# A four-layer image kernel: spline weights loaded and prepared earlier, value ranges taken per image, and sent rows counted on two semaphores

## The chip, the cores and the metric

The kernel runs on one core of one Trainium2 chip. The metric is the device time of one execution in microseconds (us). The engines are TensorE (PE; its weight loads are PEld), VectorE (DVE), ScalarE (ACT), GpSimd (POOL) and SyncE (SP), which here only issues DMAs.

## The reference

The input x is 8 images of 32 x 32 positions with 128 channels, so 8192 tokens. Four layers follow each other. Each adds two things to x: a mixer of the normalised x, and a mixture of experts of the again normalised sum. The mixers are a fractal measure (L0), an involution (L1), a spline network (L2) and an attention without softmax (L3). The layer that matters here is L2. Its mixer is, with `n` the normalised x:

```
x_min, x_max = min and max of n per channel over all 8192 tokens
u      = (n - x_min) / (x_max - x_min + 1e-7)
bases  = hat functions of u on a grid of 9 knots
spline = einsum(bases, spline_weight * spline_scaler)      # 128 x 128 x 9
out    = silu(bn_base(n @ base_weight)) + bn_spline(spline)
```

The minimum and the maximum go over all images, so no token's bases can be computed before the last image is normalised. Every layer's experts take each token's best expert (L0) or its best two (L1, L2, L3) of 8 (16 in L3), run a two-step network on it, and add the weighted results.

## The kernel before, in words

`build` (L2294) runs constants, then for each layer `norm_mixer` and the layer's mixer, then `finish`. Each of these is a block of its own: five programs, one per engine, that start together and are waited for together at the end, so a block's start stands behind its slowest engine.

`norm_mixer` (L249) first brings back the results of the layer before: SP loads them image by image (L276), GpSimd adds each token's two results (L284), VectorE adds them to the residual and takes statistics (L299, L301). When all 8 images are in, one square root on ScalarE (L332) and a reciprocal follow. Then the images are normalised in tiles of 128 tokens, 8 tiles per image: VectorE takes six (L313), ScalarE two (L339). TensorE turns each image so that channels lie on partitions (L326), and ScalarE copies it into `k.ch` (L347, or L349 where the image has no border).

`mixer_spline` (L1860) opens the next block. SP loads eight vectors of 128 numbers (`load_columns`, L1239), the base weight, the spline weight and its scaler, and waits for them; only then come the bias columns, the gate and the experts' weights. VectorE writes some constants (L1929, L1931), waits for the loads, scales the weights (L1935), derives from the 9 knots one slope and three bends (L1937 to L1941), a level at zero (L1943), the batch norm factors (L1949 to L1953) and the combined weights (L1955). TensorE turns these (L2026). VectorE then takes the channel's minimum and maximum over all 8192 tokens in two reductions (L1958, L1959), and works out the range, its inverse and the three bend positions (L1960 to L1963). After them come the bends of image 0 (`bends`, L1971) on VectorE and ScalarE's scaled copies of the turned weights (L2006), and TensorE starts on the images.

While a mixer works on image b, `Router` handles image b-1: its sum and norm, the choice of experts, and the slots into which its rows go (`place`, with the end of each image at L693 and L695). GpSimd then sends the rows to a buffer in device memory by indirect DMA, one DMA per tile and choice, 16 per image with two choices (`send_tile`, L795). The slots have two buffers, for even and odd images. All sends of a layer count on one semaphore, `rows_sent`, and `send` waits at the end of each image until all of them have landed:

```
    def send(self, pool, b):
        self.slots_known(pool, b)
        for t in range(TPB):
            self.send_tile(pool, b, t)
        pool.wait_ge(*self.when("rows_sent", 16 * TPB * self.K * (b + 1)))
```

`Experts` then works through tiles of 128 dispatched rows, 136 of them in L1 and L2, 144 in L3, in loops whose body spells out 16 tiles (`tiles`, L929 to L961). SP loads a tile's rows into one of 16 places (`load`, L965), and for this waits until the tile 16 before has been returned. TensorE turns it (L1004) and does the two products (L1012, L1022), ScalarE the activation (L1079, L1082), VectorE copies and weights the result (L1120, L1126, L1145), and GpSimd returns it by an indirect DMA (L1214). The last image is routed in between: its sends stand in GpSimd's program before the returns of certain tiles (in L2 from the thirteenth on, in L1 from the tenth on), and VectorE places it and plans the second part of the tiles between other tiles. SP writes pad rows (L493) between the loads of the third sixteen, then loads the second table (L500), waits for all rows sent and all pads, and goes on with the loads.

## Time and profile before

| | |
|---|---|
| runs | 2334.99, 2335.71, 2338.59 us (median 2335.71) |
| profiled execution, its own time | 2337.0 us |
| its span | 2335.2 us |
| granted TensorE clock, mean | 0.874 |
| busy: PE / PEld | 1749.2 us (75%) / 1376.5 us (59%) |
| busy: DVE / ACT / POOL | 1550.6 us (66%) / 1174.8 us (50%) / 983.7 us (42%) |
| DMA | 153.81 MB, 66 GB/s over the span |

The times are of whole executions. The span is what the hardware profiler saw from the first to the last instruction, 1.8 us less than the execution's own time. Busy shares are means over stages with different limits. In a timeline, each line has the start, the length, the engine, the line of the kernel, the operation, output and inputs, the shape and the number of instructions merged into it. In brackets stands how long the engine was idle before it, and what ended this.

### The profile page before, as it was taken

The page shows a single profiled execution, that of the slowest core. Times are in us where ns is not written, and L with a number is a line of the kernel's source. Part 1 is how long each engine was busy: PE and PEld are TensorE (multiplying, and loading weights), DVE is VectorE, ACT ScalarE, POOL GpSimd, SP SyncE. Part 2 cuts the span into 40 slices and gives each one's busy share as a digit, 9 for nine tenths or more (in the row PEclk, how much of TensorE's full clock was granted, in tenths as well). Part 3 has the DMA queues.
Part 4 walks back from the last instruction along what each step waited for, and adds up shares of the span by engine and source line. Part 5 has one row for each costly group of instructions (what it writes and reads, how often), then busy time and mean ns, then how long its engine had stood idle before and what let it go on. Part 6 is the DMA issues. An engine that isn't in the chain of part 4 may idle for free. (4 is left out here: it accounts for less than half of the span.)

```text
span 2335.2 us, 46315 instructions
## 1 busy us (share of the span) xinstructions
PE 1749.2 (75%) x10980; PEld 1376.5 (59%) x10981; DVE 1550.6 (66%) x4683; ACT 1174.8 (50%) x2635; POOL 983.7 (42%) x969
## 2 busy tenths in 40 slices
PE   1488666993588888999952566779719999888992
PEld 1133566893344345999951344667617777787992
DVE  6898886786577776654437676646576777754554
ACT  2445776893333334776642233546635444455661
POOL 0000233552013435764442077677640365466662
PEclk9799766997699999999985788779959999989996
DMA  2002002222200002232242012233243011123326
GB/s 74 1 0 60 26 27 56 78 69 83 74 12 26 32 23 65 76 93 63 60 136 75 11 51 76 64 94 102 78 145 109 19 38 33 52 70 96 92 77 220
DMA packets 183551, 153.81 MB, mean 66 GB/s; under 512 B 40290, under 2 KB 162818, under 8 KB 183358
## 3 DMA queue, kind: packets, MB, share of 16 engines
q1 hardware_dynamic: 153406, 92.37, 14.6%
q0 software_dynamic: 29952, 59.26, 7.5%
q8 instruction: 74, 1.21, 0.2%
q14 instruction: 119, 0.97, 0.2%
HBM read 85.33 MB, written 68.79 MB: 66 GB/s over the span
## 5 line engine op out<-in xcount | busy, mean ns | idle before, releaser
L1214 POOL DMA_INDIRECT returned<-rows_second_choice x488 | 482.4, 989 | 312.1 <-DVE rows_second_choice L1145 111.5
L1012 PE MATMUL psum<-rows_first_choice 128*128 128x128 f32 x3360 | 473.0, 282 | 8.1 <-DVE rows_first_choice L1126 8.1
L1022 PE MATMUL psum<-expert_weights,rows_first_choice 128*128 x2784 | 427.7, 290 | 61.7 <-ACT rows_first_choice L1079 17.3
L1012 PEld LDWEIGHTS psum<-rows_first_choice 128*128 128x128 f32 x3360 | 431.5, 199 | 10.1 <-DVE rows_first_choice L1126 9.9
L1022 PEld LDWEIGHTS psum<-expert_weights,rows_first_choice 128*128 128x128 f32 x2784 | 361.5, 197 | 99.8 <-issue 93.1
L795 POOL DMA_INDIRECT dispatched<-rows_first_choice,slot x192 | 191.6, 998 | 519.3 <-DVE rows_second_choice L695 409.2
L1079 ACT ACTIVATE rows_first_choice<-psum,bias_columns 128x128 f32<-128x128 f32 x1104 | 323.5, 368 | 171.9 <-PE psum L1012 153.8
L795 POOL DMA_INDIRECT dispatched<-rows_second_choice,slot x192 | 193.5, 1008 | 58.5 <-issue 58.2
L1120 DVE COPY rows_first_choice<-expert_weights 128x512 f32 (+1 forms) x272 | 105.8, 389 | 144.5 <-PE psum L1012 120.6
L326 PE MATMUL psum<-identity,rows_first_choice 128*128 128x128 f32 x256 | 41.5, 320 | 201.8 <-DVE rows_first_choice L313 190.3
L1145 DVE SCALAR_TENSOR_TENSOR rows_second_choice<-psum,rows_second_choice,rows_first_choice 128x128 f32<-128x128 f32 x344 | 119.4, 347 | 103.9 <-PE psum L1022 101.1
L795 POOL DMA_INDIRECT dispatched<-rows_first_choice,expert_weights x64 | 62.1, 970 | 267.5 <-DVE rows_first_choice L693 250.1
L1062 ACT ACTIVATE rows_first_choice<-expert_weights 128x512 f32 x216 | 136.8, 634 | 50.0 <-issue 49.9
L326 PEld LDWEIGHTS psum<-identity,rows_first_choice 128*128 128x128 f32 x256 | 34.9, 167 | 207.7 <-DVE rows_first_choice L313 190.7
L1126 DVE COPY rows_first_choice<-psum 128x128 f32<-128x128 f32 x488 | 137.2, 282 | 13.6 <-PE psum L1004 12.4
L1004 PE MATMUL psum<-identity,rows_second_choice 128*128 128x128 f32 x488 | 137.5, 283 | 7.9 <-DMA rows_second_choice<-dispatched 7.6
L1082 ACT ACTIVATE rows_first_choice<-rows_first_choice,rows_second_choice 128x128 f32 x344 | 141.2, 410 | 0.0
L1132 DVE TENSOR_TENSOR rows_first_choice<-rows_first_choice,psum 128x256 f32<-128x256 f32 x144 | 60.6, 421 | 113.8 <-ACT rows_first_choice L1072 106.5
L2214 PE MATMUL psum<-channel_major 128*128 128x512 f32 x256 | 131.7, 598 | 1.2 <-ACT channel_major L2132 1.2
L2148 ACT ACTIVATE att_work<-psum 128x512 f32<-128x512 f32 x128 | 73.1, 596 | 90.0 <-PE psum L2214 84.1
L2223 PEld LDWEIGHTS psum<-rows_second_choice,rows_first_choice 128*128 128x128 f32 x680 | 88.7, 191 | 47.0 <-issue 34.9
L2223 PE MATMUL psum<-rows_second_choice,rows_first_choice 128*128 128x128 f32 x680 | 90.3, 276 | 5.4 <-DVE rows_first_choice L2182 5.4
(369 smaller groups left out, 3274.6 us busy)
## 6 DMA issues: line engine op xcount, KB each, us to landing
rows_second_choice<-dispatched SPq DMA_DIRECT2D x488, 65.0 KB
expert_weights<-returned SPq DMA_DIRECT2D x12, 1024.0 KB, 10.3
rows_second_choice<-returned SPq DMA_DIRECT2D x8, 1024.0 KB, 10.6
returned<-rows_second_choice POOLq DMA_INDIRECT x488
expert_weights<-in_L_ffn_w SPq DMA_DIRECT2D x3, 2048.0 KB, 8.3
residual<-in_x SPq DMA_DIRECT2D x8, 512.0 KB, 7.2
rows_first_choice<-returned SPq DMA_DIRECT2D x4, 1024.0 KB, 8.9
out<-residual SPq DMA_DIRECT2D x8, 512.0 KB, 6.0
```

What stands on the lines that cost most here:

```text
L795: pool.indirect_dma_start(out=self.k.dispatched, out_offset=bass.IndirectOffsetOnAxis(ap=self.slot[:, b % 2, c, t:t + 1], axis=0), in_=sel ...
L1004: pe.transpose(k.ps[:, self.PSX + u % 2, 0:P], self.rt[:, u, 0:C], k.ident[:]).then_inc(self.s["x_turned"].h, 1)
L1012: ins = pe.matmul(k.ps[:, self.PSH + u % 2, j * P:(j + 1) * P], self.wc[:, u % 2, j * P:(j + 1) * P], self.xt[:, u % 2, :], start=True, st ...
L1022: ins = pe.matmul(self.result_bank(u), self.gs[:, u % self.HB, j * P:(j + 1) * P], self.second[:, bass.ds(e, 1), j, :].rearrange("p a c -> ...
L1062: act.activation(self.wc[:, u % 2, :], self.first[:, bass.ds(e, 1), :].rearrange("p a f -> p (a f)"), ACT.Copy).then_inc(self.s["w_copied" ...
L1079: ins = act.activation(self.hs[:, u % self.HB, cols], k.ps[:, self.PSH + u % 2, cols], f["act"], bias=self.bcol[:, bass.ds(e * self.J + j, ...
L1082: act.activation(self.wb[:, u % 4, :], self.b2rows[:, bass.ds(e, 1), :].rearrange("p a c -> p (a c)"), ACT.Copy, scale=self.rt[:, u, C + 1 ...
L1126: dve.tensor_copy(self.xt[:, u % 2, :], k.ps[:, self.PSX + u % 2, 0:P]).then_inc(self.s["x_copied"].h, 1)
L1145: ins = dve.scalar_tensor_tensor(out=self.ys[:, u, :], in0=self.result_bank(u), scalar=weight, in1=self.wb[:, u % 4, :], op0=ALU.mult, op1 ...
L1214: pool.indirect_dma_start(out=k.returned[0:N * self.K, :], out_offset=bass.IndirectOffsetOnAxis(ap=self.rt[:, u, C:C + 1].bitcast(I32), ax ...
L2214: pe.matmul(k.ps[:, g % 4, :], xft[:, b * IMG + j * P:b * IMG + (j + 1) * P], xft[:, b * IMG + h * BANK:b * IMG + (h + 1) * BANK], start=T ...
L2223: ins = pe.matmul(k.ps[:, 4 + h, t * P:(t + 1) * P], r2[g % 3][:, t * P:(t + 1) * P], val[:, b, j * P:(j + 1) * P], start=(j == 0 and t == ...
```

## The change

Four things are changed.

1. A new class `SplineWeights` holds the spline mixer's weights and small vectors. They are allocated ahead of layer 1's mixer, the large ones in a part of `rows_second_choice` behind image 6's start. Its `load` issues the eleven DMAs on SP; it is given to layer 1's `Experts` as `load_next`, which calls it behind the last tile's load and waits there for the landing.
2. Layer 2's `norm_mixer` is given these weights. VectorE does the arithmetic on them (`prepare`) ahead of the residual additions, ScalarE the two roots first, and TensorE turns the combined weights first.
3. In that block ScalarE normalises tiles 1, 2, 4, 5 and 7 of each image and VectorE the other three. VectorE takes the minimum and the maximum of each image once it is copied, two images behind its own tiles. The mixer only reduces the 8 minima and 8 maxima.
4. `rows_sent` becomes `even_sent` and `odd_sent`. `send` no longer waits for its own rows, but before an image for those of the image two before it. Whoever waited for all rows waits for both semaphores.

```diff
-def norm_mixer(k, layer):
+def norm_mixer(k, layer, spline=None):
...
+    by_scalar = (1, 2, 4, 5, 7) if spline else (3, 7)
...
+            if spline:
+                spline.prepare(dve)
             for b in range(B):
                 ch = Chain(dve, s["norm_step"], s["norm_step"].base + b * per)
...
+            def image_range(b):
+                dve.wait_ge(*when("turned_copied", b + 1))
+                spline.image_range(dve, b)
+
             for b in range(B):
-                for t in (b * TPB + j for j in range(TPB) if j % 4 != 3):
+                for t in (b * TPB + j for j in range(TPB) if j not in by_scalar):
                     ins = dve.tensor_scalar(k.xn[:, t, :], k.x[:, t, :], k.mean[:, t:t + 1], k.rstd[:, t:t + 1],
                                             ALU.subtract, ALU.mult)
                 ins.then_inc(s["norm_most"].h, 1)
+                if spline and b >= 2:
+                    image_range(b - 2)
+            if spline:
+                image_range(B - 2)
+                image_range(B - 1)
...
         def _(pe):
+            if spline:
+                spline.turn(pe)
...
         def _(act):
+            if spline:
+                spline.roots(act)
...
-                for t in range(b * TPB + 3, (b + 1) * TPB, 4):
+                for t in (b * TPB + j for j in by_scalar):
...
+    def sent(self, images, parity):
+
+        return self.when(("even_sent", "odd_sent")[parity], 16 * TPB * self.K * ((images + 1 - parity) // 2))
+
+    def all_sent(self, eng, images):
+        for parity in range(2):
+            eng.wait_ge(*self.sent(images, parity))
...
             if b >= 2:
-                dve.wait_ge(*self.when("rows_sent", 16 * TPB * K * (b - 1)))
+                dve.wait_ge(*self.sent(b - 1, b % 2))
...
-                in_=self.rows[c][:, b * TPB + t, :], in_offset=None).then_inc(self.s["rows_sent"].h, 16)
+                in_=self.rows[c][:, b * TPB + t, :],
+                in_offset=None).then_inc(self.s[("even_sent", "odd_sent")[b % 2]].h, 16)
...
     def send(self, pool, b):
         self.slots_known(pool, b)
+        if b >= 2:
+            pool.wait_ge(*self.sent(b - 1, b % 2))
         for t in range(TPB):
             self.send_tile(pool, b, t)
-        pool.wait_ge(*self.when("rows_sent", 16 * TPB * self.K * (b + 1)))
...
         route.load_table(sp, 0)
-        sp.wait_ge(*route.when("rows_sent", 16 * TPB * self.K * route.first_images))
+        route.all_sent(sp, route.first_images)
...
         route.load_table(sp, 1)
-        sp.wait_ge(*route.when("rows_sent", 16 * TPB * self.K * B))
+        route.all_sent(sp, B)
...
         for t in range(self.T // RING * RING, self.T):
             load(t, t % RING)
+        if self.load_next:
+            self.load_next(sp)
...
                 route.slots_known(pool, B - 1)
+                pool.wait_ge(*route.sent(B - 2, (B - 1) % 2))
...
+class SplineWeights:
...
+    def load(self, sp):
+        i, sem = self.k.ins, self.s["spl_loaded"]
+        load_columns(sp, sem, self.vec, [i[f"L2_conv_bn_{a}_{b}"] for a in ("base", "spline")
+                                         for b in ("gamma", "beta", "mean", "var")])
+        sp.dma_start(self.base_w[:], i["L2_conv_base_weight"]).then_inc(sem.h, 16)
+        sp.dma_start(self.spw[:], i["L2_conv_spline_weight"]).then_inc(sem.h, 16)
+        sp.dma_start(self.scl[:], i["L2_conv_spline_scaler"]).then_inc(sem.h, 16)
+        sp.wait_ge(*self.when("spl_loaded", 16 * 11))
...
+    def image_range(self, dve, b):
+        image = self.k.ch[:, b * IMG:(b + 1) * IMG]
+        dve.tensor_reduce(self.ranges[:, 0, b:b + 1], image, AX.X, ALU.min).then_inc(self.s["spl_ranged"].h, 1)
+        dve.tensor_reduce(self.ranges[:, 1, b:b + 1], image, AX.X, ALU.max).then_inc(self.s["spl_ranged"].h, 1)
...
-            ch.note(dve.tensor_reduce(rng[:, 0:1], k.ch[:, 0:N], AX.X, ALU.min))
-            ch.link(dve.tensor_reduce(rng[:, 1:2], k.ch[:, 0:N], AX.X, ALU.max))
+            dve.wait_ge(*weights.when("spl_ranged", 2 * B))
+            ch.note(dve.tensor_reduce(rng[:, 0:1], weights.ranges[:, 0, :], AX.X, ALU.min))
+            ch.link(dve.tensor_reduce(rng[:, 1:2], weights.ranges[:, 1, :], AX.X, ALU.max))
```

`prepare`, `roots` and `turn` hold the same operations on the weights as `mixer_spline` had, in the same order, with their scratch room in `rows_first_choice`.

## Rows read from the trace of the kernel before

**Rows 1.** The head of the page: the whole span.
```profile
span 2335.2 us, 46315 instructions
```

**Rows 2.** Windows: stretch, length, busy of PE, PEld, DVE, ACT, POOL, clock, DMA.
```profile
1265.00:1300.00 35.00, 1.19 (x5) 0.79 (x5) 26.06 (x36) 1.87 (x8) 0.00 (x0) 0.51 0.29 82
...
1600.00:1660.00 60.00, 57.38 (x419) 47.64 (x418) 37.70 (x139) 42.22 (x139) 44.84 (x46) 1.00 0.37 103
```

**Rows 3.** Timeline of VectorE, norm block of L2 and the mixer's preparation.
```profile
1218.87 3.36 DVE L299 TENSOR_TENSOR residual<-residual,expert_weights 128x1024 f32<-128x1024 f32 x1 [17.35 <-POOL expert_weights L284]
...
1248.92 12.39 DVE L313 TENSOR_SCALAR rows_first_choice<-residual,mean,rstd 128x128 f32<-128x128 f32 x48
1265.48 0.29 DVE L1929 MEMSET hats_at_zero<- 128x1 f32 x9 [4.17 <-PEq L264]
...
1273.83 1.36 DVE L1935 TENSOR_TENSOR spline_w<-spline_w,spline_scaler 128x1152 f32<-128x1152 f32 x1 [7.98 <-DMA spline_scaler<-in_L_conv_spline_scaler]
...
1280.66 8.68 DVE L1958 TENSOR_REDUCE channel_range<-channel_major 128x1 f32<-128x8192 f32 x1
1289.26 8.68 DVE L1959 TENSOR_REDUCE channel_range<-channel_major 128x1 f32<-128x8192 f32 x1
1297.97 0.16 DVE L1960 TENSOR_TENSOR channel_range<-channel_range 128x1 f32<-128x1 f32 x1
...
1298.73 2.08 DVE L1971 TENSOR_SCALAR expert_weights<-channel_major,bends 128x1024 f32<-128x1024 f32 x3
```

**Rows 4.** Timeline of ScalarE in the same norm block.
```profile
1249.04 1.65 ACT L339 ACTIVATE rows_first_choice<-residual,four_variances,rstd 128x128 f32<-128x128 f32 x4 [0.95 <-DVE four_variances L309]
1252.61 1.03 ACT L349 ACTIVATE channel_major<-psum 128x1024 f32<-128x1024 f32 x1 [1.92 <-PE psum L326]
1253.53 0.87 ACT L339 ACTIVATE rows_first_choice<-residual,four_variances,rstd 128x128 f32<-128x128 f32 x2
1254.31 1.03 ACT L349 ACTIVATE channel_major<-psum 128x1024 f32<-128x1024 f32 x1
...
1264.12 1.02 ACT L349 ACTIVATE channel_major<-psum 128x1024 f32<-128x1024 f32 x1 [0.29 <-PE psum L326]
```

**Rows 5.** Timelines of SP and GpSimd, end of L1 and start of the norm block.
```profile
1129.24 45.70 SPq L965 DMA_DIRECT2D rows_second_choice<-dispatched  x24
1206.79 5.78 SPq L276 DMA_DIRECT2D expert_weights<-returned  x4
...
1216.51 2.33 POOL L284 TENSOR_TENSOR expert_weights<-expert_weights 128x1024 f32<-128x1024 f32 x1 [13.73 <-issue]
```

**Rows 6.** Timeline of GpSimd in L2: sends and the first returns.
```profile
1335.90 1.42 POOL L795 DMA_INDIRECT dispatched<-rows_first_choice,slot  x1 [95.04 <-DVE rows_second_choice L695]
...
1467.23 0.96 POOL L795 DMA_INDIRECT dispatched<-rows_first_choice,slot  x1 [1.60 <-DMA dispatched<-rows_second_choice,slot]
...
1489.37 1.00 POOL L1214 DMA_INDIRECT returned<-rows_second_choice  x1 [2.10 <-DMA dispatched<-rows_second_choice,slot]
...
1505.54 1.00 POOL L1214 DMA_INDIRECT returned<-rows_second_choice  x1 [0.30 <-issue]
1506.85 1.07 POOL L795 DMA_INDIRECT dispatched<-rows_first_choice,slot  x1 [0.30 <-issue]
```

**Rows 7.** Timeline of VectorE in L2: image 6's slots, the twelfth tile's result.
```profile
1462.41 0.17 DVE L695 TENSOR_TENSOR rows_second_choice<-weight_sum,exponentials 128x8 f32<-128x8 f32 x1
...
1502.14 0.35 DVE L1145 SCALAR_TENSOR_TENSOR rows_second_choice<-psum,rows_second_choice,rows_first_choice 128x128 f32<-128x128 f32 x1
```

**Rows 8.** Timeline of SP in L2: tile loads around the pads.
```profile
1538.72 1.66 SPq L965 DMA_DIRECT2D rows_second_choice<-dispatched  x2
...
1563.24 109.22 SPq L965 DMA_DIRECT2D rows_second_choice<-dispatched  x88
```

**Rows 9.** Timeline of GpSimd in L1: the ninth return.
```profile
948.59 0.98 POOL L1214 DMA_INDIRECT returned<-rows_second_choice  x1 [1.48 <-DVE rows_second_choice L1145]
```

**Rows 10.** Timeline of ScalarE in L1's experts: the first of two such gaps.
```profile
1086.03 1.14 ACT L1079 ACTIVATE rows_first_choice<-psum,bias_columns 128x128 f32<-128x128 f32 x4 [5.38 <-issue]
```

More of the change, by code:

```diff
@@ L882, with __init__ @@
     HB = 4
-    def __init__(self, k, layer, ctx, route):
+    def __init__(self, k, layer, ctx, route, load_next=None):
         nc, f = k.nc, FFN[layer]
+        self.load_next = load_next
         self.k, self.layer, self.f, self.route, self.tail = k, layer, f, route, TAILS[layer]
@@ L1611, in mixer_fractal, with mixer_involution @@
     route.done()
-def mixer_involution(k):
+def mixer_involution(k, load_next):
     nc, i = k.nc, k.ins
@@ L1872, in mixer_spline @@
+def mixer_spline(k, weights):
+    nc = k.nc
+    BENDS, TERMS = weights.BENDS, weights.TERMS
+    base_w, bn, bend, level = weights.base_w, weights.bn, weights.bend, weights.level
+    names = ("spl_v", "spl_wcopied", "spl_shift", "spl_basis", "spl_level", "spl_base", "spl_used", "spl_silu", "spl_mixed")
     s = {n: k.sem(n) for n in names}
@@ L1904, in _ @@
         def _(sp):
-            load_columns(sp, s["spl_loaded"], vec, [i[f"L2_conv_bn_{a}_{b}"] for a in ("base", "spline")
-                                                    for b in ("gamma", "beta", "mean", "var")])
-            sp.dma_start(base_w[:], i["L2_conv_base_weight"]).then_inc(s["spl_loaded"].h, 16)
-            sp.dma_start(spw[:], i["L2_conv_spline_weight"]).then_inc(s["spl_loaded"].h, 16)
-            sp.dma_start(scl[:], i["L2_conv_spline_scaler"]).then_inc(s["spl_loaded"].h, 16)
-            sp.wait_ge(*when("spl_loaded", 16 * 11))
             ex.sync_early(sp)
@@ L1946, in _ @@
-            dve.wait_ge(*when("spl_root", 2))
-            for j in range(2):
-                g, bt, mn = (vec[:, 4 * j + a:4 * j + a + 1] for a in range(3))
-                ch.link(dve.reciprocal(bn[:, j, 1:2], bn[:, j, 0:1]))
-                ch.link(dve.tensor_tensor(bn[:, j, 1:2], bn[:, j, 1:2], g, ALU.mult))
-                ch.link(dve.tensor_tensor(bn[:, j, 2:3], bn[:, j, 1:2], mn, ALU.mult))
-                ch.link(dve.tensor_tensor(bn[:, j, 2:3], bt, bn[:, j, 2:3], ALU.subtract))
-            ch.note(dve.scalar_tensor_tensor(out=level[:, 0:1], in0=level[:, 0:1], scalar=bn[:, 1, 1:2], in1=bn[:, 1, 2:3],
-                                             op0=ALU.mult, op1=ALU.add))
@@ L1999, in _ @@
         def _(act):
-            act.wait_ge(*when("spl_loaded", 16 * 11))
-            for j in range(2):
-                act.activation(bn[:, j, 0:1], vec[:, 4 * j + 3:4 * j + 4], ACT.Sqrt, bias=k.eps3).then_inc(s["spl_root"].h, 1)
             act.wait_ge(s["spl_v"].h, s["spl_v"].base + k.spline_pre)
-            act.wait_ge(*when("spl_wturned", 1))
+            act.wait_ge(*weights.when("spl_wturned", 1))
             for t in range(TERMS):
-                act.activation(spt[:, t, :], k.ps[:, 4, t * P:(t + 1) * P], ACT.Identity,
+                act.activation(spt[:, t, :], k.ps[:, weights.BANK, t * P:(t + 1) * P], ACT.Identity,
                                scale=rng[:, 2:3]).then_inc(s["spl_wcopied"].h, 1)
@@ L2023, in _ @@
         def _(pe):
-            pe.wait_ge(*when("spl_combined", 1))
-            for t in range(TERMS):
-                ins = pe.transpose(k.ps[:, 4, t * P:(t + 1) * P], combined[:, t, :], k.ident[:])
-            ins.then_inc(s["spl_wturned"].h, 1)
             pe.wait_ge(*when("spl_wcopied", TERMS))
@@ L2273, in build @@
         constants(k)
-        mixers = [mixer_fractal, mixer_involution, mixer_spline, mixer_attention]
-        for layer in range(4):
-            norm_mixer(k, layer)
-            mixers[layer](k)
+        norm_mixer(k, 0)
+        mixer_fractal(k)
+        norm_mixer(k, 1)
+        with ExitStack() as spline_ctx:
+            weights = SplineWeights(k, spline_ctx)
+            mixer_involution(k, weights.load)
+            norm_mixer(k, 2, weights)
+            mixer_spline(k, weights)
+        norm_mixer(k, 3)
+        mixer_attention(k)
         finish(k)
```

109 lines of the change are left out of this document (71 added, 38 removed).

## The prediction

> **What bounds the kernel now.** I read the page's head first: one core, 2335.2 us of span [rows 1]. The profiled execution took 2337.0 us, 1.8 more than its span; the median of the runs is 2335.71, 1.3 below it. The sum is made against the profiled execution and carried over to the median as it is. No engine is full over the whole span, so what a part of the change is worth must be read stage by stage, and the second view is the table of windows around the third layer (L2), where nearly all of the change lies [rows 2]. In it two things stand out. From 1265 to 1300 us TensorE does 1.19 us of work in 35 and GpSimd nothing: that is the spline mixer's preparation, and the whole kernel stands behind it. From 1600 to 1660 GpSimd returns 46 tiles, one per 1.30 us, while TensorE is busy for 57.38 of 60: there the expert stage is limited by two engines at once.
>
> The third view is VectorE's timeline of the preparation [rows 3]. The reader is to see one unbroken sequence: block start at 1265.48, 7.98 us of idling until the last weight lands, 6.8 us of small work on the weights (1273.83 to 1280.66), two reductions of all 8192 columns, four small operations (0.76 us, 1297.97 to 1298.73), and then the first bends. Nothing else runs, so 33.25 us from block start to bends is critical.
>
> **Part 1: weights loaded behind layer 1's tiles.** Eleven DMAs go onto SP's queue behind the last tile load. SP issues its last tile load of layer 1 by 1174.94 (1129.24 + 45.70) and is next needed at 1206.79 [rows 5]. From the mixer's start to the landing of the last of the eleven went 8.4 us, 1265.48 to 1273.83 [rows 3]; the hole has 31.9. Cost 0. If the cover were gone, at most those 8.4 us would return. The load ring's tiles are issued ahead, so no tile load stands behind them.
>
> **Part 2: the weights' arithmetic in the norm block.** VectorE now idles 17.35 us until 1218.87, waiting for the first image's rows to come back and be added by GpSimd [rows 3]. The block starts at about 1206.8, SP's first issue [rows 5]. Twelve memsets 0.4 us, then 6.8 to 6.9 us of arithmetic: done at 1214.1, 4.8 us before VectorE is wanted, 2.4 us before GpSimd's first addition at 1216.51 [rows 5]. ScalarE's two roots and TensorE's four transposes run while both are idle; bank 4 is not used by the norm. Cost 0, gain: 1265.48 to 1280.66, that is 15.2 us, leaves the path.
>
> The Trainium skill speaks of what happens if the cover is missed: in its page SBUF — State Buffer, section on SBUF's two separate sides, a VectorE operation with two SBUF inputs and a GpSimd operation that reads SBUF exclude each other for their whole duration. The trace agrees in that the first residual addition, beside GpSimd's second, took 3.36 us [rows 3].
>
> **Part 3: the norm block's new split and the ranges.** ScalarE normalises 5 tiles of an image, not 2; VectorE 3, not 6, and takes each image's minimum and maximum. ScalarE's pace: two tiles take 0.78 us from start to start (1253.53 to 1254.31), so 0.39 each; two tiles and a copy of an image take 1.70 (1252.61 to 1254.31), so the copy's share is 0.92 [rows 4]. From 1249.04: ten tiles 3.9 us, first copy from 1253.0 to 1254.0; then 5 x 0.39 + 0.92 = 2.87 us per image; the seventh copy starts at 1270.2, the eighth is over by 1272.4 after its transposes.
>
> VectorE: a tile costs 12.39/48 = 0.26 us [rows 3], so 24 tiles 6.2 us. A reduction of 1024 columns isn't in the trace. From below it costs 8.68/8 = 1.08; from above 1024/1152 of the 1.36 us of L1935, 1.21 [rows 3]. I take 1.13: 1024 columns at 1.06 ns, 0.14 us fixed (L1935's 1.36 less 1152 x 1.06), less the 0.08 by which neighbours overlap (1280.66 to 1289.26 is 8.60, not 8.68). Sixteen make 18.1. VectorE does three images' tiles by 1251.3, waits for the first copy until 1254.0, and then is the later of the two engines: 1248.92 + 6.2 + 18.1 + 2.7 = 1275.9. Both ends of the reduction's cost give 1275.1 and 1277.2.
>
> The skill's page VectorE: DVE Perf Modes, section on the TRN2 errata, speaks against cutting one large reduction into eight: SBUF operations pay a fixed extra latency per instruction. By its (N+151)/0.96 a reduction would take 1.22 us and sixteen 19.6, so the block would end at 1277.4; no run here shows this shape.
>
> After the block: about 0.3 us to the next (it was 1265.14, the end of the last copy, to 1265.48) [rows 3, 4], two reductions over 8 numbers some 0.3 together, then the same four operations, 0.76. Bends start at 1277.3 and not at 1298.73: **21.4 us gained**. What is late next is nothing new: ScalarE's copies of the turned weights wait for the same ranges as before. The gate's and experts' loads now start with the block, at 1276.3, rather than once the spline weights had landed, about 1273.8, and are wanted from 1300 on. Cost 0, and at most a microsecond or two if the gate's weights were late.
>
> **Part 4: two semaphores for sent rows.** Before, GpSimd stood after each image's sends until all had landed. Layer 0, 1 and 3: images come slower than they are sent, so the wait hides, except the one before the first returned tile (about 2.1 us less 0.3 of normal spacing). In layer 1 the ninth tile then waits 1.48 us for VectorE's result anyway [rows 9], so nothing is left; I cost layers 0 and 3 at 0 by the same pattern, at most 1.8 us each.
>
> Layer 2 is different. There GpSimd is never idle by more than these waits: sends from 1335.90, a gap at each of the six image changes, 1.60 us before image 6, and 2.10 before the first return at 1489.37 [rows 6]. Sixteen sends take 1489.37 - 2.10 - 1467.23 = 20.0 us. Image 6's slots were ready at 1462.58 [rows 7] but its sends began at 1467.23. Without the waits they begin at 1462.9, end at 1482.9, and the first return comes at 1483.3, 6.1 us early. But from the first to the twelfth return took 16.2 us [rows 6], so the twelfth would go at 1499.5, and its result is only there at 1502.49, after VectorE has placed image 7 and planned the second half [rows 7]. So it goes at 1502.8, not 1505.54: **2.7 us** remain. They do pass on: image 7's sends (from 1506.85) set the pace of returns, these free the ring's tiles, SP's loads follow them until 1540 and from there SP's own chain of pads leads to the second table and the load at 1563.24 [rows 6, 8]. SP's and VectorE's new waits are for things long past.
>
> Sum: 21.4 + 2.7 = 24.1. From 2337.0 to 2312.9; against the median 2335.71, **2311.6**.
>
> **Rivals.**
> (a) The full 6.1 us pass through, because image 7's work on TensorE and VectorE also moves up: 27.5, 2308.2. For it: GpSimd has no other idle time in the layer. Against: that work waits for nothing from GpSimd. 0.10.
> (b) Nothing of the 2.7 comes through: GpSimd's sends now begin together with the bends on VectorE, and the one send that did so took 1.42 us, not 0.96 [rows 6]; or TensorE is the bound later. 21.4, 2314.3. 0.11.
> (c) The arithmetic doesn't fit under the return of rows, or the loads don't fit behind the tiles: 3 to 8 us back, 2315 to 2320. 0.05.
> (d) Slower. In layer 1 ScalarE twice stood for 5.4 us at a jump back of the expert loop, waiting for nothing in the program ("issue") [rows 10]; in layers 2 and 3 it never does. If this hangs on where the loop's code lies, the change moves it: ScalarE's program is longer by 24 activations ahead of both loops. These loops jump back 4 times in layer 2 and 5 in layer 3. All nine would cost 9 x 5.4 = 48.6 us less 24.1: 2360. It decides from the fifth jump on (27.0 > 24.1). All or most: 0.04. One to three of them, 2317 to 2328: 0.04.
> (e) The change doesn't do what it says: something else holds the mixer's start or the time comes back in the expert stage where two engines are full; within 4.7 us of 2335.7. 0.03.
>
> **How the numbers follow.** My forecast has 0.63, the rivals the rest. 0.2% of this time, 4.7 us, is about what a measurement of this kernel can tell from no change. Faster by more: 0.63 + 0.10 + 0.11 + 0.05 + 0.04 = 0.93; same 0.03; slower 0.04. Low end: rival (a) 2308.2 less the reduction at its cheap end (0.8) and 1.8 us of layer 0 or 3, 2305.6, rounded to 2305. High end: the forecast with the dear reduction (1.3), without the 2.7, and with one reload of 5.4: 2321.
>
> **What would show it.** Right: in the changed profile VectorE's spline arithmetic lies in the gap before the first residual addition, which starts no later than 12.1 us after the block; bends follow the norm block's end by 1.4 us and come 28.5 us after the normalisation starts, where it was 49.8; GpSimd's first send of each layer 2 image comes 0.4 us after its slots; its first return comes 6 us earlier against the mixer's start, its first send of image 7 under 3. Wrong: reductions of over 1.25 us, VectorE late for the first addition, sends of 1.4 us throughout, ScalarE gaps over 4 us at jumps in layers 2 or 3, or an expert stage longer by what the mixer gained.

## The result and the profile after

| | before | after |
|---|---|---|
| median of the runs beside each other | 2337.15 us | 2304.15 us |
| ratio, 95% interval | | 0.9859 [0.9845, 0.9874] |
| profiled execution, its span | 2335.2 us | 2301.3 us |
| norm block of L2, first DMA to first bends | 91.9 us | 70.7 us |
| first bends to image 6's slots | 163.8 us | 161.2 us |
| image 6's slots to the next norm block | 229.8 us | 222.9 us |
| next norm block to the end | 642.9 us | 639.9 us |

The table's stretches run from event to event. The norm block of L2 starts at SP's first load of returned rows; "image 6's slots" is the end of VectorE's row that writes the weights of its first choices (L693 before, L718 after). The row of the second choices, which the prediction took, ends 0.08 us later.

The change gains 33.0 us by the medians. The forecast was 24.1 and 2311.6; the range reached down to 2305, and the result lies 0.85 us below it. A second comparison gave 2303.55 against 2334.55, ratio 0.9874 [0.9857, 0.989], so 31.0. Of the table's rows the first three differences are 21.3, 2.6 and 6.9 us. The last row is the spread of profiles: kernels that keep all the old waits had 638.6 and 640.1 there (warm_before, warm_before2).

The head of the page of after:

```profile
span 2301.3 us, 46320 instructions
```

SP's timeline at the end of L1, which answers to [rows 5]: the eleven loads follow the last tile at once, and the last is issued over 25 us before SP is next needed.

```profile
1174.98 1.40 SPq L1270 DMA_DIRECT2D spline_vectors<-in_L_conv_bn_base_gamma  x1
...
1180.70 0.42 SPq L1933 DMA_DIRECT2D rows_second_choice<-in_L_conv_spline_scaler  x1
1206.72 8.75 SPq L277 DMA_DIRECT2D expert_weights<-returned  x5
```

VectorE's timeline of the norm block and the start of the mixer, which answers to [rows 3]:

```profile
1206.80 0.29 DVE L1944 MEMSET hats_at_zero<- 128x1 f32 x9 [5.32 <-PEq L1669]
...
1213.76 0.48 DVE L1971 TENSOR_SCALAR rows_second_choice<-rows_second_choice,spline_bn 128x512 f32<-128x512 f32 x1
1218.70 3.35 DVE L302 TENSOR_TENSOR residual<-residual,expert_weights 128x1024 f32<-128x1024 f32 x1 [4.46 <-POOL expert_weights L285]
...
1254.08 1.22 DVE L1988 TENSOR_REDUCE image_ranges<-channel_major 128x1 f32<-128x1024 f32 x1 [2.94 <-ACT channel_major L366]
1255.21 1.21 DVE L1989 TENSOR_REDUCE image_ranges<-channel_major 128x1 f32<-128x1024 f32 x1
1256.34 0.85 DVE L321 TENSOR_SCALAR rows_first_choice<-residual,mean,rstd 128x128 f32<-128x128 f32 x3
...
1274.82 1.21 DVE L1989 TENSOR_REDUCE image_ranges<-channel_major 128x1 f32<-128x1024 f32 x1
1276.36 0.16 DVE L2038 TENSOR_REDUCE channel_range<-image_ranges 128x1 f32<-128x8 f32 x1 [0.32 <-PEq L265]
...
1277.38 2.08 DVE L2051 TENSOR_SCALAR expert_weights<-channel_major,bends 128x1024 f32<-128x1024 f32 x3
```

The weights' arithmetic is over 4.46 us before the first residual addition (and 2.1 before GpSimd's first addition at 1216.34). The residual addition has not moved against the block's start (12.0 us; 12.1 before). From the first copy on VectorE has no idle time until the block ends. Its bends come 1.35 us after the block's last reduction, 28.6 us after the normalisation starts, where the forecast had 1.4 and 28.5.

GpSimd's timeline at image 6 of L2, which answers to [rows 6]:

```profile
1438.89 0.96 POOL L820 DMA_INDIRECT dispatched<-rows_first_choice,slot  x1 [0.47 <-DVE rows_second_choice L720]
...
1457.98 0.96 POOL L820 DMA_INDIRECT dispatched<-rows_second_choice,slot  x1 [0.30 <-issue]
1459.24 1.00 POOL L1245 DMA_INDIRECT returned<-rows_second_choice  x1 [0.30 <-issue]
1460.54 1.00 POOL L1245 DMA_INDIRECT returned<-rows_second_choice  x1 [0.31 <-issue]
...
1474.09 0.98 POOL L1245 DMA_INDIRECT returned<-rows_second_choice  x1 [0.91 <-DVE rows_second_choice L1175]
1475.38 0.97 POOL L820 DMA_INDIRECT dispatched<-rows_first_choice,slot  x1 [0.31 <-issue]
```

GpSimd now waits for the slots (released by VectorE's L720), not for its own rows, and its first send comes 0.34 us after image 6's slots at 1438.55. Counted from image 6's slots, the first return comes 6.2 us earlier than before (20.7 after 26.9), the first send of image 7 7.5 us earlier (36.8 after 44.3). The forecast had 6.1 and 2.7. The twelfth return, at 1474.09, is the only one among these that waits for VectorE, and it loses 0.6 us.

### The profile page after: what moved, and what is told of

The parts are those of the page before. It is cut to its first block and busy times, and to the rows that moved or that the text cites. A ratio compares the mean times of both kernels' runs of the same rounds, so it can differ in the third digit from the quotient of the medians.

```text
span 2301.3 us, 46320 instructions
## 1 busy us (share of the span) xinstructions
PE 1745.5 (76%) x10964; PEld 1375.2 (60%) x10981; DVE 1545.8 (67%) x4675; ACT 1183.7 (51%) x2659; POOL 981.1 (43%) x969
## 3 DMA queue, kind: packets, MB, share of 16 engines
q8 instruction: 74, 1.21, 0.2%
## 5 line engine op out<-in xcount | busy, mean ns | idle before, releaser
L820 POOL DMA_INDIRECT dispatched<-rows_second_choice,slot x192 | 187.7, 978 | 58.5 <-issue 58.2
L1156 DVE COPY rows_first_choice<-psum 128x128 f32<-128x128 f32 x488 | 137.4, 282 | 10.9 <-PE psum L1034 10.2
L2296 PEld LDWEIGHTS psum<-rows_second_choice,rows_first_choice 128*128 128x128 f32 x680 | 88.7, 191 | 47.0 <-issue 34.9
```

The source lines that it names most:

```text
L820: pool.indirect_dma_start(out=self.k.dispatched, out_offset=bass.IndirectOffsetOnAxis(ap=self.slot[:, b % 2, c, t:t + 1], axis=0), in_=sel ...
L1156: dve.tensor_copy(self.xt[:, u % 2, :], k.ps[:, self.PSX + u % 2, 0:P]).then_inc(self.s["x_copied"].h, 1)
L2296: ins = pe.matmul(k.ps[:, 4 + h, t * P:(t + 1) * P], r2[g % 3][:, t * P:(t + 1) * P], val[:, b, j * P:(j + 1) * P], start=(j == 0 and t == ...
```

## The experiments

"Stage 1" is the stretch from the norm block's start to the first bends, "stage 2" from there to image 6's slots, "stage 3" from there to the next norm block; all in L2, from each kernel's profile. In each set the kernel before ran beside them.

| kernel | median us | ratio, 95% interval | stage 1 | stage 2 | stage 3 |
|---|---|---|---|---|---|
| before | 2334.4 to 2337.2 | | 91.9 | 163.8 | 229.8 |
| after | 2304.15 | 0.9859 [0.9845, 0.9874] | 70.7 | 161.2 | 222.9 |
| after_again | 2303.55 | 0.9874 [0.9857, 0.989] | 70.7 | 161.1 | 222.5 |
| sems_only | 2328.42 | 0.9974 [0.9964, 0.9985] | 91.9 | 163.8 | 221.5 |
| all_waits | 2314.49 | 0.9915 [0.9898, 0.9931] | 70.7 | 160.9 | 230.8 |
| first_waits | 2311.85 | 0.9904 [0.9888, 0.9921] | 70.6 | 161.2 | 229.4 |
| last_wait | 2308.23 | 0.9895 [0.9879, 0.9912] | 70.5 | 161.3 | 224.1 |
| whole_range | 2311.5 | 0.9905 [0.9888, 0.9921] | 76.7 | 162.1 | 221.4 |
| old_split | 2306.86 | 0.9883 [0.9866, 0.9899] | 74.0 | 161.2 | 222.0 |
| load_in_norm | 2313.79 | 0.9912 [0.9896, 0.9929] | 80.8 | 161.2 | 222.1 |
| long_prepare | 2325.15 | 0.9962 [0.9949, 0.9974] | 88.4 | 163.9 | 221.9 |
| warm_before | 2334.68 | 1.0001 [0.9988, 1.0014] | 91.8 | 163.3 | 231.5 |
| warm_before2 | 2331.63 | 0.999 [0.9981, 1.0] | 92.2 | 159.8 | 230.1 |
| warm_after2 | 2303.67 | 0.9871 [0.9855, 0.9888] | 70.4 | 161.3 | 222.0 |

Stage 3 tells the two kinds apart at once: 229.4 to 231.5 where the waits at the image changes stand, 221.4 to 222.9 where no old wait is left; last_wait, with the one ahead of the first return, has 224.1.

### The sends: where did 6.9 us come from, when 2.7 was the forecast?

Two theories stood against each other. A: the whole cost of the waits passes on. B, the forecast's: the twelfth tile's result caps it.

**sems_only.** The kernel before with part 4 alone: `even_sent` and `odd_sent`, and no wait behind an image's own sends.

> The kernel before with the two semaphores alone. Two theories stand after the changed profile. A: the semaphores are worth all that GpSimd is ahead in L2, 4.4 us at image 6's sends, 1.8 at the first return, and 1.9 more at the second return, which no longer stands 2.2 us; the twelfth result is in time for this. Then image 7's first send comes about 8 us earlier against the bends' start than before, and with up to 2 us in L3 the kernel takes 2327 to 2329, 8 to 10 under before (2337.15). B, as predicted: the twelfth result caps it, 2.7 us, 2334.4; the rest of the 33 us then comes from the spline part.

Stage 3 fell from 229.8 to 221.5, 8.3 us; the median by 6.1 (2328.42 beside 2334.52), for which theory A had 8 to 10 and B 2.7. The part is worth this much without any help from the rest of the change. In the eight profiles without the old waits stage 3 lies between 221.4 and 222.9, so its price is known to about 1.5 us.

**all_waits, first_waits, last_wait.** The changed kernel with the wait for its own rows put back, on the two semaphores, behind every image, behind images 0 to 5 alone, or behind image 6 alone:

```diff
         for t in range(TPB):
             self.send_tile(pool, b, t)
+        self.all_sent(pool, b + 1)        # all_waits
...
+        if b < B - 2:                     # first_waits; last_wait has b == B - 2
+            self.all_sent(pool, b + 1)
```

> The changed kernel with GpSimd's wait for its own rows back at the end of each image (both semaphores). Theory A: 8 to 10 us over the changed kernel (2304.15), 2312 to 2314, and the bends still start within 0.3 us of where they do now against the norm block's start. Theory B: 2.7 over it, 2306.9. If the parts add up, this and the run of the semaphores alone are equally far from their neighbours.

> The changed kernel with the waits back behind images 0 to 5, none ahead of the first return. Theory A: image 6's sends in L2 begin some 4.4 us later and all that follows too, without either gap at the returns: 2308 to 2309. Theory B: capped by the twelfth result, at most 1 us over the changed kernel, 2305.

> The changed kernel with the wait back at one place only, behind image 6's sends and ahead of the first return. If the 2.2 us ahead of the second return belong to this wait, both gaps come back in every layer: first return of L2 1.8 us later, second 3.7, and the whole some 3.7 to 5 over the changed kernel, 2308 to 2309. If the second gap has another cause, it stays away and the whole is 1.8 over, 2306.

All of the waits cost 7.9 us of stage 3, those between images alone 6.5, the one ahead of the first return 1.2. By the medians the three kernels stand 10.3, 7.7 and 4.1 us above the changed kernel's 2304.15; A had expected 8 to 10, some 4.4 and 3.7 to 5, so it missed first_waits. So the cost is in the main an accumulated lag. In the kernel before, sixteen sends and their spacing take 20.3 us (16 x 1.27), with the gap of 1.6 to the next image 21.9, and an image comes every 21.2 (127.0 us for six). Each standstill pushes the following image's sends back, until image 6 starts 4.7 us after its slots.

The waits put back on two semaphores are longer than the old ones. The kernel before has gaps of 1.6 to 1.8 us at the image changes behind the first; in first_waits and all_waits every second gap is 2.1 to 2.4, and image 6's sends begin 7.3 and 7.4 us after its slots, not 4.7. So 6.5 and 7.9 are too high as prices of the old waits. GpSimd's row of image 6's first send in first_waits:

```profile
1446.90 1.02 POOL L820 DMA_INDIRECT dispatched<-rows_first_choice,slot  x1 [2.36 <-issue]
```

B falls: with the waits between images put back the twelfth return came 6.5 us later than in the changed kernel (from image 6's slots: 42.0 after 35.5).

GpSimd's timeline of last_wait shows what else the wait ahead of the returns does:

```profile
1458.84 0.96 POOL L820 DMA_INDIRECT dispatched<-rows_second_choice,slot  x1 [0.31 <-issue]
1461.89 1.00 POOL L1247 DMA_INDIRECT returned<-rows_second_choice  x1 [2.10 <-DVE rows_second_choice L1177]
1464.71 0.99 POOL L1247 DMA_INDIRECT returned<-rows_second_choice  x1 [1.82 <-issue]
1466.01 0.98 POOL L1247 DMA_INDIRECT returned<-rows_second_choice  x1 [0.30 <-issue]
```

There are two gaps and not one: 2.10 us ahead of the first return, which is the wait, and 1.82 ahead of the second, for which the profile names nothing in the program ("issue"). In the kernel before, the second is 2.2 us in L1, L2 and L3; there the profile names VectorE's L1145 in L1 and L2, but in L2 the second tile's result had been ready since 1476.49, 16 us earlier; in the changed kernel and in first_waits both gaps are gone in these layers (0.30). Behind a wait between images the next send follows after 0.3 us.

### The norm block: is each part worth what the sum said?

Theory C, in these expectations, is that the mixing is shorter after the change because TensorE enters it at a higher clock; the section after this one is on it.

**whole_range.** The changed kernel with part 3 undone: tiles 3 and 7 for ScalarE, no ranges in the norm block, two reductions of 8192 columns in the mixer.

```diff
-    by_scalar = (1, 2, 4, 5, 7) if spline else (3, 7)
+    by_scalar = (3, 7)
...
-            dve.wait_ge(*weights.when("spl_ranged", 2 * B))
-            ch.note(dve.tensor_reduce(rng[:, 0:1], weights.ranges[:, 0, :], AX.X, ALU.min))
-            ch.link(dve.tensor_reduce(rng[:, 1:2], weights.ranges[:, 1, :], AX.X, ALU.max))
+            ch.note(dve.tensor_reduce(rng[:, 0:1], k.ch[:, 0:N], AX.X, ALU.min))
+            ch.link(dve.tensor_reduce(rng[:, 1:2], k.ch[:, 0:N], AX.X, ALU.max))
```

> The changed kernel with part 3 undone: ScalarE normalises tiles 3 and 7 again, no ranges in the norm block, and the mixer takes two reductions of all 8192 columns. By my sum part 1 and 2 are worth 15.2 us and part 3 6.2 us, so the first bends should come 70.7 + 6.1 = 76.8 us after the norm block's start, and the whole time should rise by 6.1 us over the changed kernel. Theory C (clock) adds up to 1.7 to 2.6 us of slower mixing, because TensorE stands idle for 17 us again ahead of its first product: 6.1 to 8.7 in all, and bends to image 0's slots back near 36.8. Rival D (layout, loads): mixing stays at 35.1 and the rise is 6.1. A third outcome, under 4 us, would say that the ranges per image were worth less than the sum says.

Stage 1 is 76.7 us: parts 1 and 2 took 15.2 off the 91.9 and part 3 another 6.0, as summed (15.2 and 6.2). Stage 2 grew by 1.0, less than the 1.7 to 2.6 that theory C allowed, and image 0's slots came 35.6 us after the bends, between the rival's 35.1 and theory C's 36.8. The median stands 7.3 above the changed kernel.

**old_split.** Only the first two lines of that diff; VectorE takes 48 tiles and the ranges.

> The changed kernel with only the split of the normalisation undone: VectorE does six tiles of an image, ScalarE two; the ranges per image stay. VectorE is the later engine at the block's end, so 24 more tiles of 0.26 us, 6.2 us, lie on it; of these part is taken out of its waits for the first copy (2.7 us in the sum). Expected: bends 3.5 us later against the norm block's start than in the changed kernel (70.7 to 74.2), whole time 3.5 us longer. Rival: if ScalarE's copies, and not VectorE, had set the end (the last copy ended 3 us before VectorE's last reduction), nothing to 1 us.

Stage 1 grew by 3.3 us and the median by some 3. VectorE is the later engine, and moving tiles to ScalarE is worth the 6.2 us of the tiles less the wait for the first copy.

**load_in_norm.** Part 1 undone: the eleven loads are issued at the start of the norm block.

```diff
         def _(sp):
+                if spline:
+                    spline.load(sp)
...
-        sp.wait_ge(*self.when("spl_loaded", 16 * 11))
...
-            mixer_involution(k, weights.load)
+            mixer_involution(k, None)
```

> The changed kernel with part 1 undone alone: the eleven loads are issued by SP at the start of layer 2's norm block, ahead of the loads of the returned rows, and not behind layer 1's last tile. By the preparation of the kernel before, the last of the eleven lands about 8 us after the first is issued, the arithmetic of 6.8 us then ends some 15 us after the block's start instead of 7.4, and the loads of rows behind them are issued 3 to 4 us later. VectorE's first residual addition came 11.9 us after the block's start. Theory: bends come 3 to 7 us later (70.7 to 74 to 78), because both the arithmetic and the returned rows are late, and the time rises by as much. Rival: the rows' way over GpSimd takes up both, since the residual additions wait for it anyway: under 2 us. Third, as in the run with the longer preparation: the arithmetic falls beside GpSimd's additions, each blocks the other, and 8 us or more appear.

The third outcome: stage 1, from the first of the eleven at 1207.93, is 80.8, 10.1 us longer, and the median 10.2 longer than the changed kernel beside it. VectorE's timeline:

```profile
1216.36 1.36 DVE L1951 TENSOR_TENSOR rows_second_choice<-rows_second_choice 128x1152 f32<-128x1152 f32 x1 [7.99 <-DMA rows_second_choice<-in_L_conv_spline_scaler]
...
1221.10 0.16 DVE L1965 RECIPROCAL spline_bn<-spline_bn 128x1 f32<-128x1 f32 x1
1221.29 2.10 DVE L1966 TENSOR_TENSOR spline_bn<-spline_bn,spline_vectors 128x1 f32<-128x1 f32 x1
1223.42 2.27 DVE L1967 TENSOR_TENSOR spline_bn<-spline_bn,spline_vectors 128x1 f32<-128x1 f32 x1
1225.72 2.27 DVE L1968 TENSOR_TENSOR spline_bn<-spline_vectors,spline_bn 128x1 f32<-128x1 f32 x1
1228.03 0.16 DVE L1965 RECIPROCAL spline_bn<-spline_bn 128x1 f32<-128x1 f32 x1
1228.23 0.16 DVE L1966 TENSOR_TENSOR spline_bn<-spline_bn,spline_vectors 128x1 f32<-128x1 f32 x1
1228.42 2.33 DVE L1967 TENSOR_TENSOR spline_bn<-spline_bn,spline_vectors 128x1 f32<-128x1 f32 x1
...
1231.24 2.47 DVE L1972 TENSOR_SCALAR rows_second_choice<-rows_second_choice,spline_bn 128x512 f32<-128x512 f32 x1
```

And GpSimd's beside it:

```profile
1220.24 7.74 POOL L287 TENSOR_TENSOR expert_weights<-expert_weights 128x1024 f32<-128x1024 f32 x3 [16.30 <-DMA expert_weights<-returned]
1228.39 2.34 POOL L287 TENSOR_TENSOR expert_weights<-expert_weights 128x1024 f32<-128x1024 f32 x1 [0.41 <-DMA expert_weights<-returned]
```

An operation on one number per partition with two operands takes 0.16 us, and 2.10 to 2.33 while GpSimd adds; the reciprocal with one operand takes 0.16 even then, and the two-operand one at 1228.23 takes 0.16 in GpSimd's gap from 1227.98 to 1228.39. One instruction with a single tensor, the 128x512 at 1231.24, was held up too: 2.47 us beside an addition, 0.48 in the changed kernel. The Trainium skill, SBUF — State Buffer, section on SBUF's two separate sides, describes this as an exclusive lock between a two-input VectorE operation and a GpSimd operation that reads SBUF, held for the whole instruction. The trace agrees in both directions: none of the held-up instructions is much longer than one addition (2.34 us), and GpSimd's first three additions, the first of them started beside a 128x1152 of VectorE (L1959), took 7.74 us where three of 2.34 make 7.0.

The five held-up instructions lost 10.3 us together. But the run also moved something else: the loads of the returned rows stand behind the eleven, 5.1 us later, and GpSimd's first addition came 12.3 us after the block's first issue, not 9.6. The 10.1 us of the stage hold both effects, and no run here parts them.

**long_prepare.** The changed kernel with eight more multiplications of 128x1152 in `prepare`:

```diff
+        for _ in range(8):
+            ch.settle()
+            ch.note(dve.tensor_tensor(junk.rearrange("p (c t) -> p c t", t=KN), spw[:],
+                                      scl[:].unsqueeze(2).to_broadcast([P, C, KN]), ALU.mult))
```

> The changed kernel with eight more multiplications of the shape of the spline weight by its scaler (128x1152, 1.36 us each) in the preparation ahead of the residual additions, 11 us in all (with their waits 11 to 12). VectorE idled 4.46 us there, so this much is hidden and 6.5 to 7.5 us should appear: bends at 77 to 78 us after the norm block's start, whole time 6.5 to 7.5 us longer. Rival: because VectorE's arithmetic and GpSimd's additions would now fall together, and the first residual addition beside one of GpSimd's took 3.35 us where the others take about 1.1, they slow each other: then over 8 us. Second rival: the residual additions wait image by image for GpSimd, so a late start is caught up again and under 4 us appear.

Stage 1 grew by 17.7 us (the median by 21.0, with 2.7 more from stage 2), where 6.5 to 7.5 would have been the arithmetic alone: the eight took 19.19 us together instead of 11, and four of the small ones 2.06 to 2.26 each.

```profile
1212.81 19.19 DVE L1963 TENSOR_TENSOR rows_first_choice<-rows_second_choice 128x1152 f32<-128x1152 f32 x8
1231.92 0.15 DVE L1968 RECIPROCAL spline_bn<-spline_bn 128x1 f32<-128x1 f32 x1
1232.11 2.10 DVE L1969 TENSOR_TENSOR spline_bn<-spline_bn,spline_vectors 128x1 f32<-128x1 f32 x1
```

In the changed kernel GpSimd's first addition starts 9.6 us after the block, at 1216.34. Up to there arithmetic was free in these runs; behind it a two-operand instruction took about as long as one addition, however small it was, as long as GpSimd had no gap. (The expectation gives about 1.1 us for the other residual additions; the rows have 1.21 to 1.69.)

### The mixing: why 2.6 us shorter?

Windows of the first 14 us of mixing, before and then after; the third number from the end is TensorE's granted clock (1.00 is 2.4 GHz, 0.50 is 1.2 GHz):

```profile
1298.70:1305.70 7.00, 5.36 (x8) 2.68 (x9) 2.65 (x15) 3.38 (x6) 0.00 (x0) 0.50 0.01 2
1305.70:1312.70 7.00, 6.95 (x15) 2.62 (x13) 0.00 (x0) 1.54 (x2) 0.00 (x0) 0.92 0.00 0
```

```profile
1277.40:1284.40 7.00, 5.40 (x10) 2.77 (x11) 2.63 (x15) 3.67 (x7) 0.00 (x0) 0.62 0.49 103
1284.40:1291.40 7.00, 5.55 (x14) 2.10 (x12) 1.34 (x2) 1.22 (x1) 0.00 (x0) 1.00 0.55 203
```

The clock leaves its lower level earlier after the change. Over all fourteen profiles the first image follows this clock, and so does stage 2 but for warm_after2:

| granted clock, first 7 us of mixing | kernels | bends to image 0's slots | stage 2 |
|---|---|---|---|
| 0.50 | before, sems_only, long_prepare, warm_before | 36.8 | 163.3 to 163.9 |
| 0.55 | whole_range | 35.6 | 162.1 |
| 0.61 to 0.64 | after, after_again, all_waits, first_waits, last_wait, old_split, load_in_norm | 35.0 to 35.2 | 160.9 to 161.3 |
| 1.00 | warm_before2 | 33.5 | 159.8 |
| 1.00 | warm_after2 | 33.6 | 161.3 |

**warm_before** and **warm_before2.** The kernel before with 60, then 138 turns of the identity matrix ahead of TensorE's wait for the scaled weights, their results unused:

```diff
+            for t in range(138):
+                pe.transpose(k.ps[:, 7, (t % 4) * P:(t % 4 + 1) * P], k.ident[:], k.ident[:])
             pe.wait_ge(*when("spl_wcopied", TERMS))
```

> The kernel before, with 60 turns of the identity matrix given to TensorE just ahead of its wait for the four scaled spline weights (into a bank nothing else uses then), so that it works through the stretch in which it stood idle. The question is where the 1.7 us (to image 0's slots) and 2.6 us (to image 6's) come from by which the changed kernel's mixing is shorter, counted from the first bends. Theory C, the clock: TensorE enters the mixing at a higher granted clock; then bends to image 0's slots falls from 36.8 to about 35.1 us, bends to image 6's slots from 163.8 to 161 to 162.5, and the whole time by 1.5 to 2.6 us. Rival D, it is the memory layout (weights and scratch in other places) or the loads that start earlier: both stretches stay within 0.3 us of 36.8 and 163.8, and the whole time within 1 us of the kernel before.

> The kernel before with 138 turns of the identity matrix ahead of TensorE's wait for the scaled spline weights, where the run before this one had 60: those ended 9.4 us before the first product, the clock was back at 0.50 by then, and nothing was told apart. At the 0.107 us that the last of the 60 took, 138 end about 1 us before the scaled weights come. Theory C (the clock at which the mixing starts sets its length): granted clock 0.9 to 1.0 in the first 7 us of the mixing where it was 0.50, bends to image 0's slots 33.5 to 35.5 instead of 36.8, bends to image 6's slots at most 161.5 instead of 163.8. Rival: the mixing does not hang on the first 7 us of clock, 36.8 and 163.8 stay within 0.4.

The 60 missed their aim: they ended 9.4 us too early, the clock stood at 0.50 again when mixing began, and both stretches were near those of before (36.8 and 163.3). The 138 reached it, and windows of warm_before2 show the full clock:

```profile
1299.60:1306.60 7.00, 5.43 (x16) 2.50 (x14) 2.63 (x15) 4.90 (x7) 0.00 (x0) 1.00 0.00 0
1306.60:1313.60 7.00, 5.55 (x20) 2.81 (x19) 2.86 (x4) 0.00 (x0) 0.00 (x0) 1.00 0.00 0
```

Bends to image 0's slots fell from 36.8 to 33.5, stage 2 from 163.8 to 159.8. The median fell by 2.9 us, with an interval that reaches up to no change (0.9981 to 1.0). So the clock at the start is enough to move stage 2 by more than the change did. The rival, layout or earlier loads, falls with long_prepare: it has the changed kernel's layout and loads, and its mixing took 36.8 and 163.9, at 0.50 and 0.91 in the first two windows. Why the clock rises earlier in the changed kernel stays open: TensorE's work of the last 30 us before the bends is the same in long_prepare and in the changed kernel, the granted clock of the last 10 is 0.50 in both, and only in the 7 us behind the bends do they part (0.50 and 0.62).

**warm_after2** and **after_again.** The changed kernel with TensorE kept at work: 36 turns of the identity ahead of the first image's turns, 8 behind those of images 1 to 6, 36 behind the last, 16 ahead of the scaled weights; and the changed kernel itself.

```diff
             if spline:
                 spline.turn(pe)
+                pe.wait_ge(*when("norm_step", (B - 1) * per))
+                warm(36)
...
                 ins.then_inc(s["turned"].h, 1)
+                if spline and b:
+                    warm(8 if b < B - 1 else 36)
```

> The changed kernel with TensorE kept at work from the end of the statistics on: 36 turns of the identity before the first image's turns, 8 behind those of each of images 1 to 6, 36 behind the last, 16 ahead of the scaled spline weights. Theory C: the granted clock is near 1.00 when mixing starts (0.62 in the changed kernel's first 7 us), image 0's slots come 33.5 to 34.5 us after the bends instead of 35.1, and the whole time falls by 0.5 to 1.5 us against the changed kernel beside it. Rival: the extra turns delay the copies of the first images, VectorE gets its ranges later, and the norm block grows by 1 to 2 us, so that nothing is won or the time is longer by up to 2 us.

> The changed kernel itself, once more, beside the others of this call: 2304 us, and as a second profile the same stage lengths as the first within 0.3 us in layer 2 (norm block's start to bends 70.7, bends to image 6's slots 161.2, image 6's slots to the next norm block 222.9 with up to 2.5 of scatter, as the runs so far show in that stretch).

Image 0's slots came 33.6 us after the bends, 1.4 earlier, and image 6's at 161.3, no earlier at all; 2303.67 against 2303.55. The windows of warm_after2 tell where it was given back: behind the first 20 us the clock falls, while TensorE still has its work of images 0 and 1. In the second and third window below it is 0.82 and 0.54; the changed kernel has 1.00 and 0.61 in the same windows from its bends. Image 1's slots are level again, 55.5 us after the bends for 55.4.

```profile
1291.40:1299.80 8.40, 8.40 (x21) 3.64 (x20) 6.89 (x28) 2.79 (x3) 0.00 (x0) 1.00 0.00 0
1299.80:1306.00 6.20, 3.12 (x25) 2.76 (x23) 1.59 (x8) 3.25 (x3) 0.00 (x0) 0.82 0.00 0
1306.00:1314.80 8.80, 5.93 (x23) 3.82 (x24) 8.29 (x26) 1.54 (x2) 2.42 (x2) 0.54 0.02 8
```

No version that was run beats the changed kernel.

## Why the prediction was right or wrong

**Parts 1 to 3: right.** 21.4 us were forecast, 21.3 measured (91.9 to 70.7), and whole_range splits them as the sum did. The reduction of 1024 columns took 1.21 us, at the upper of the two bounds, but the next starts 1.13 after it, which is the number that the sum used: the last one ended at 1276.03 for 1275.9. The Trainium skill, VectorE: DVE Perf Modes, section on the TRN2 errata, gives (N+151)/0.96 ns for an addition of two fp32 tensors, not for a reduction; the prediction's 1.22 us is an estimate worked out from it. The trace agrees with it for one reduction (1.21 to 1.22 us); taken sixteen times in a row it gave a block end of 1277.4, 1.4 too late, since it has no overlap in it.

**Part 4: wrong, and the larger of two errors that together took the result out of the range.** The forecast let the first return come 6.1 us earlier (6.2 measured) and then held the twelfth back for its result "only there at 1502.49", which left 2.7. VectorE's timeline of the kernel before has these rows in that stretch:

```profile
1498.11 0.34 DVE L1145 SCALAR_TENSOR_TENSOR rows_second_choice<-psum,rows_second_choice,rows_first_choice 128x128 f32<-128x128 f32 x1
...
1502.14 0.35 DVE L1145 SCALAR_TENSOR_TENSOR rows_second_choice<-psum,rows_second_choice,rows_first_choice 128x128 f32<-128x128 f32 x1
```

The row at 1502.14, on which the step stood [rows 7], is the thirteenth tile's result. The twelfth's is the one before it, ready at 1498.45, ahead of the plan and not behind it, and a return at 1499.5 would have found it. Counting the rows of L1145 from the first tile of the layer shows it, and was not done. The thirteenth's return stands behind the first two sends of image 7 and waits just 0.2 us longer than its neighbours after the change. So the full 6.1 passed. With stage 3's measured 6.9 in place of 2.7 the forecast would have been 2307.4, still inside its range of 2305 to 2321; it took the next term as well to leave it. This has the size of rival (a), not its mechanism: image 7's slots came 34.9 us after image 6's, for 35.6 before, so that work hardly moved, and nothing needed it to.

**What stood in no term.** The second gap behind the wait, 2.2 us, went as well: the sum took over the 16.2 us from the first to the twelfth return as they stood, with the gap among them. 6.2 and 1.9 less the 0.6 that the twelfth return now waits make the 7.5 us by which image 7's sends start earlier; 6.9 are left at the end of the stage. And the mixing gave 2.6 us, through the clock by the experiments above, for which the forecast had neither a term nor a rival; 2307.4 less 2.6 is 2304.8. The forecast's 24.1 and these errors of 4.2 (6.9 less 2.7) and 2.6 make 30.9; the three stages show 30.8. What is left of the 33.0 is within the spread of the comparison (31.0 in the second).

**Rivals.** (b) and (c) needed sends of 1.4 us or late arithmetic; nearly all sends took 0.96 us (1.22 to 1.42 for the first of images 0, 4 and 5) and the arithmetic had 4.5 us to spare. load_in_norm and long_prepare show that (c), 3 to 8 us, was priced too low: there missing the cover cost 10.1 and 17.7 us, in good part because arithmetic and additions exclude each other. (d), code of ScalarE's loops: its gaps of 5.4 us stayed at two, both in L1, and none came in L2 or L3. (e) falls with the result. SP's loads behind L1's tiles cost nothing, as forecast.

**The range.** Its low end took in rival (a) and a cheap reduction, but no gain from the clock, though TensorE's clock stood at 0.51 in the very rows that were read [rows 2].

## What to carry to other kernels

A standstill at the end of each round on an engine that is nearly as slow as the rounds adds up over the rounds: price it by how far the last round starts behind its inputs, and let the gain pass unless a result is shown to be late, its row found by counting from the first. Where work is moved under a wait on VectorE, the cover for two-operand operations ended here at GpSimd's first addition, not at VectorE's own next instruction. Removing an idle stretch ahead of TensorE can also change the clock at which the next stage begins; take a bound for that from rows at either clock.

## What was unexpected of the hardware

- Behind a wait of GpSimd for its own sends, the first return was 2.1 us late and the second again, by 2.2 us (1.8 with the wait on two semaphores). The second gap came only where the wait stood ahead of returns, in L1, L2 and L3 with two choices; in L0 and behind waits between images the next gap was 0.3. The cause is open. The waits on two semaphores between images were longer at every second change (2.1 to 2.4 us for 1.6); that cause is open too.
- A VectorE operation with two operands of one number per partition took 2.06 to 2.33 us instead of 0.16 beside a GpSimd addition; a reciprocal beside it took 0.16.
- TensorE's granted clock at the start of mixing was 0.50, 0.55, about 0.62 or 1.00 in different kernels. It was worth up to 3.3 us on the first image and up to 4.0 on the stage (warm_before2), and nothing on the stage in warm_after2, where it fell to 0.54 later.
